# Attention and expert routing on one core: whole-pair slots, maxima ten pairs ahead, three stack buffers

## What is computed

```python
xl, xg = layer_norm(x, g_l, b_l), layer_norm(x, g_g, b_g)
glb   = mha(xg, ...)            # 16 heads of 8, softmax over the 256 tokens of a sequence
local = mha(xl[:, :32], ...)    # the same with its own weights, on tokens 0 to 31; 0 elsewhere
x1 = layernorm(x + local + glb)
# top-1 routing to 8 experts, capacity T/E = 1024, in token order
gates = softmax(x1 @ Wg); idx = argmax(gates); place = cumsum(one_hot(idx)) - 1
out = gates1 * (relu(x1 @ W1[idx] + b1) @ W2[idx] + b2)   # 0 for a token beyond the capacity
x = layernorm(x1 + out)
```

## Time and profile before

| | |
|---|---|
| median of three runs | 808.11 us |
| profiled execution | 806.47 us, span 804.4 us |
| attention steps 0 to 35 | 47.2 to 635 us |
| drain of the routing | to 665 us |
| expert stage | to the end |
| mean granted clock of TensorE | 0.917 |

### The profile page before, as it was taken

One profiled execution on the slowest core, in us unless ns is written; L12 is line 12 of the kernel. 1 busy time (PEld: TensorE's weight loads), 2 busy tenths in 40 slices (PEclk: granted clock), 3 DMA queues, 4 the chain that ended last, 5 costly groups with the idle time before them and its releaser, 6 DMA issues.

```text
span 804.4 us, 19344 instructions
## 1 busy us (share of the span) xinstructions
PE 698.3 (87%) x6502; PEld 352.4 (44%) x6502; DVE 571.7 (71%) x1703; ACT 489.6 (61%) x882; POOL 498.5 (62%) x1015
## 2 busy tenths in 40 slices
PE   1579779798999999999999999899999828999991
PEld 1434333343444444444444444344434415777771
DVE  5455577676988889889898898877888211666664
ACT  1335456575878677778787777777777614344340
POOL 4432323546677776777777878775765660667666
PEclk9755798888999999999999999999999958999996
DMA  3532576846254343552543534424431111343321
GB/s 89 174 127 60 158 188 141 207 108 211 63 175 145 107 154 86 156 166 83 173 142 111 155 109 138 154 75 146 128 114 51 32 29 51 103 128 95 98 76 35
DMA packets 145778, 95.36 MB, mean 119 GB/s; under 512 B 14404, under 2 KB 137885, under 8 KB 145680
## 3 DMA queue, kind: packets, MB, share of 16 engines
q1 hardware_dynamic: 139824, 85.35, 37.0%
q0 software_dynamic: 4096, 7.81, 3.0%
q10 hardware_dynamic: 1760, 0.96, 0.5%
HBM read 47.70 MB, written 45.74 MB: 116 GB/s over the span
## 4 chain that ended last, share of the span: by engine, by line
PE 62%; SPq 17%; DMA 7%; POOL 5%; issue 4%; DVE 3%; ACT 2%; POOLq 0%; ACTq 0%; DVEq 0%
PE ps_b L535 15%; PE ps_o L561 15%; SPq L328 8%; PE ps_a L1365 6%; DMA qs<-mT 5%; PE ps_b L1359 5%; SPq L357 5%; PE ps_f L476 3%; PE ps_f L481 3%; PE ps_f L471 2%; SPq L383 2%; POOL out L1479 2%; PE ps_a L512 2%; PE ps_f L1359 1%; PE ps_m L571 1%
## 5 line engine op out<-in xcount | busy, mean ns | idle before, releaser
L926 DVE TENSOR_REDUCE mx<-ps_a 128x2 f32<-128x512 f32 (+1 forms) x576 | 374.1, 656 | 119.0 <-PE ps_a L512 111.8
L759 ACT ACTIVATE prob<-ps_b 128x1024 f32<-128x1024 f32 (+1 forms) x288 | 281.1, 976 | 110.1 <-PE ps_b L535 97.0
L535 PE MATMUL ps_b<-qs,ks 59*128 59x256 bf16 (+1 forms) x1152 | 224.1, 277 | 32.1 <-DMA qs<-mT 29.6
L512 PE MATMUL ps_a<-ks,qs 56*128 56x256 bf16 (+1 forms) x1152 | 223.8, 279 | 7.2 <-DVE mx L926 4.8
L561 PE MATMUL ps_o<-prob,vp 128*32 128x256 f32 (+1 forms) x2304 | 184.8, 395 | 0.0
L535 PEld LDWEIGHTS ps_b<-qs,ks 59*128 59x128 bf16 x1152 | 67.0, 95 | 193.7 <-issue 113.5
L1153 POOL CAST mpart<-mx 128x16 bf16<-128x16 f32 x72 | 14.2, 197 | 123.5 <-DVE mx L926 123.2
L1217 POOL DMA_INDIRECT routed<-row,slot x64 | 67.3, 1051 | 31.5 <-issue 26.3
L1479 POOL DMA_INDIRECT out<-res,dest x64 | 64.8, 1013 | 34.2 <-DVE res L1454 19.1
L561 PEld LDWEIGHTS ps_o<-prob,vp 128*32 128x32 f32 x2304 | 46.8, 111 | 61.8 <-issue 54.9
L512 PEld LDWEIGHTS ps_a<-ks,qs 56*128 56x128 bf16 x1152 | 65.2, 96 | 12.9 <-DVE mx L926 8.7
(11 more groups left out here) (122 smaller groups left out, 1043.2 us busy)
## 6 DMA issues: line engine op xcount, KB each, us to landing
qs<-q_stack SPq DMA_DIRECT2D x144, 96.0 KB
ks<-k_stack SPq DMA_DIRECT2D x144, 96.0 KB
q_stack<-part SPq DMA_DIRECT2D x18, 384.0 KB
k_stack<-part SPq DMA_DIRECT2D x18, 384.0 KB
q_stack<-part SPq DMA_DIRECT2D x18, 256.0 KB
k_stack<-part SPq DMA_DIRECT2D x18, 256.0 KB
routed<-empty SPq DMA_DIRECT2D x8, 520.0 KB, 6.4
rows_sb<-routed SPq DMA_DIRECT2D x16, 260.0 KB, 3.8
```

What stands on the lines that cost most here:

```text
L512: ins = nc.tensor.matmul(ps_a[:, e, qt * S:qt * S + keys.stop - keys.start], qs[half, h, hp, qt * P:(qt + 1) * P], ks[half, h, hp, keys], ...
L535: ins = nc.tensor.matmul(ps_b[:, exp_bank(hp, e), kt * n:(kt + 1) * n], ks[half, u % 2, hp, kt * P:(kt + 1) * P], qs[half, u % 2, hp, quer ...
L759: nc.scalar.activation(prob[:, hp, 0:2 * n].rearrange("p (a n) -> p a n", a=2), src, ACT.Exp).then_inc(exp_done, 1)
L926: nc.vector.reduce_max(mx[:, u % 2, :, col], ps_a[:, e].rearrange("p (t k) -> p t k", t=2)[:, :, 0:k], axis=AX).then_inc(max_done, 1)
```

## The change

- Stacks: qs and ks have three buffers; load_stack(u) loads a whole unit with four DMAs, two steps ahead, and the mask rows are placed in four DMAs instead of eight.
- Maxima run LEAD = 10 head pairs ahead of the exponentials instead of 8.
- TensorE: the slot of a head pair is both score halves (eight matmuls), then one filler. The filler's work is spread anew over eight slots.
- Order: SP places the second maxima first, then loads the whole stack, then xr; store_stacks moves to the end of odd steps. GpSimd does scatter, bias_residual(u), split_max(u + 1, 0), the rows, the input's work, split_max(u + 1, 1), queue_places. The other engines' orders move to match.
- Small: the token counts use bf16 matmuls and accumulate the first tile's total in PSUM; oN and x1 are copied out of PSUM together (turned_T); queue_places has three operations instead of six; row numbers advance in place.

```diff
+LEAD = 10
-    qs = sb("qs", [P, 2, NH // 2, S], BF16)
-    ks = sb("ks", [P, 2, NH // 2, S], BF16)
+    qs = sb("qs", [P, 3, NH // 2, S], BF16)
+    ks = sb("ks", [P, 3, NH // 2, S], BF16)
...
-        def load_stack(u, half):
...
+        def load_stack(u):
+
+            b, h, p = u % 3, u % 2, u // 2
+            wait(sp, scores, 8 * (u - 2))
...
+                src = stack[p, :, :, h * S:(h + 1) * S].rearrange("(g e d) t n -> e (d t) g n", e=2, d=DH)
                 for e in range(2):
...
+                    sp.dma_start(dst[HALF * e:HALF * e + STACK, b], src[e]).then_inc(stack_loaded[b], 16)
...
         def step(u):
             p = first_pair(u)
-            if there(u + 1):
-                load_stack(u + 1, 1)
-            if u % 2 == 0 and u >= 2 and u // 2 + 1 < NPAIR:
-                store_stacks(u // 2 + 1)
             if there(u):
                 place_max(u, 1)
+            if there(u + 2):
+                load_stack(u + 2)
+            if there(u):
                 load_xr(u)
...
+            if there(u + 1):
+                place_max(u + 1, 0)
+            if u % 2 == 1 and (u + 1) // 2 + 1 < NPAIR:
+                store_stacks((u + 1) // 2 + 1)
             if p is not None and p + 2 < NPAIR:
                 load_x(p + 2)
-            if there(u + 2):
-                load_stack(u + 2, 0)
-            if there(u + 1):
-                place_max(u + 1, 0)
```

TensorE's filler, and its loop:

```diff
+            if hp == 0:
+                if there(u - 1):
+                    p_v(u - 1, 2, 1)
+                    p_v(u - 1, 3, 0)
                 if there(u):
+                    pe.wait_ge(mT_ready, 2 * u + 1)
                     wait(pe, y_ready, u - 1)
...
                     turn_max(u, 1)
+            if hp == 1:
+                if there(u - 1):
+                    p_v(u - 1, 3, 1)
+                inputs_early(u, 0)
+            if hp == 2:
+                inputs_early(u, 1)
...
+                    turn_o(u - 1)
+            if hp == 3:
                 if there(u):
+                    p_v(u, 0, 0)
                 if there(u + 1):
                     if there(u - 1):
                         pe.wait_ge(o_normed, u)
...
                     turn_max(u + 1, 0)
+            if hp == 4:
+                if there(u):
+                    p_v(u, 0, 1)
+                    p_v(u, 1, 0)
+                inputs_late(u, 0)
+            if hp == 5:
...
+                    count_tokens(u - 3)
+            if hp == 6:
...
         for u in range(U + 4):
             for hp in range(8):
-                for e in range(2):
-                    score_half(u, hp, e)
-                    fill(u, hp, e)
+                score_half(u, hp, 0)
+                score_half(u, hp, 1)
+                fill(u, hp)
```

VectorE (pick_place stands before the last slot's maxima) and GpSimd:

```diff
+            if at == (7, 0) and routes(u - 3):
                 pick_place(u - 3)
...
+                    if there(n // 8):
+                        take_max(n // 8, n % 8, e)
...
         def step(u):
             first, second = first_pair(u), second_pair(u)
-            if there(u):
-                split_max(u, 1)
             if routes(u - 4):
                 scatter(u - 4)
+            if there(u):
+                bias_residual(u)
+            if there(u + 1):
+                split_max(u + 1, 0)
             if routes(u - 2):
                 deviation(u - 2)
                 norm_rows(u - 2)
-            if there(u + 1):
-                split_max(u + 1, 0)
-            if routes(u - 3):
-                queue_places(u - 3)
-            if there(u):
-                bias_residual(u)
             if first is not None and first + 1 < NPAIR:
                 input_deviation(first + 1)
                 normalize_input(first + 1)
             if second is not None:
                 third_part(second)
+            if there(u + 1):
+                split_max(u + 1, 1)
+            if routes(u - 3):
+                queue_places(u - 3)
```

More of the change, by code:

```diff
@@ L771, in copy_o, with copy_turned @@
             nc.scalar.copy(oT[:], ps_o[:]).then_inc(oT_ready, 1)
-        def copy_oNT(u):
-            act.wait_ge(oN_turned, u + 1)
-            wait(act, projected, u)
-            nc.scalar.copy(oNT[:], ps_m[:, 0:S]).then_inc(oNT_ready, 1)
-        def copy_x1T(u):
-            g = batch(u)
-            act.wait_ge(x1_turned, g + 1)
-            wait(act, logits_ready, g)
-            nc.scalar.copy(x1T[:], ps_m[:, S:2 * S]).then_inc(x1T_ready, 1)
+        def copy_turned(u):
+            first, end = (0 if there(u - 1) else S), (2 * S if routes(u - 2) else S)
+            if there(u - 1):
+                act.wait_ge(oN_turned, u)
+                wait(act, projected, u - 1)
+            if routes(u - 2):
+                act.wait_ge(x1_turned, batch(u - 2) + 1)
+                wait(act, logits_ready, batch(u - 2))
+            nc.scalar.copy(turned_T[:, first:end], ps_m[:, first:end]).then_inc(turned_copied, 1)
         def norm_again(u):
@@ L813, in copy_counts @@
             act.wait_ge(counted, g + 1)
-            wait(act, places_ready, g)
-            nc.scalar.copy(count[:].rearrange("p a t e -> p (a t e)"), ps_m[:, 0:4 * E]).then_inc(counts_copied, 1)
+            wait(act, place_chain.sem, place_chain.steps * g)
+            nc.scalar.copy(count[:].rearrange("p a e -> p (a e)"), ps_m[:, 0:3 * E]).then_inc(counts_copied, 1)
         def step(u):
@@ L879, in _ @@
         copy_bv()
+        for g in range(3):
+            nc.scalar.activation(row[:, g, :, D + 1], c["tokid"][:], ACT.Copy, bias=float(g * S)).then_inc(row_numbered, 1)
         copy_max(0, 0)
@@ L1022, in fill @@
             first, second = first_pair(u), second_pair(u)
-            then = second + 2 if second is not None and second + 2 < NPAIR else None
+            early = second + 2 if second is not None and second + 2 < NPAIR else None
+            late = first + 1 if first is not None and AHEAD + 1 < first + 1 < NPAIR else None
             at = (hp, e)
-            if at == (0, 1):
+            if at == (0, 0):
                 if there(u - 2):
@@ L1047, in fill @@
+            if at == (2, 0):
+                if routes(u - 3):
+                    expert_mask(u - 3)
+                if routes(u - 2):
+                    mean_variance(u - 2)
+                if late is not None:
+                    input_stats(late, (2, 3))
+            if at == (3, 0) and there(u - 1):
                 invert_denominators(u - 1)
-            if at == (4, 1) and there(u - 1):
                 norm_o(u - 1)
-            if at == (5, 0) and then is not None:
-                input_stats(then, (0, 1))
@@ L1052, in fill @@
[L1052 to L1068 removed]
+            if at == (4, 0):
+                if second is not None:
+                    take_rest_k(second)
+                if late is not None:
+                    input_variance(late)
@@ L1251, in _ @@
         split_max(0, 0)
+        split_max(0, 1)
         for u in range(U + 4):
```

297 lines of the change are left out of this document (135 added, 162 removed).

## The result

The change makes the kernel slower: 1018.89 us (median of 4 runs, 1017.52 to 1020.1) against 807.48 us for the kernel before beside it, a ratio of 1.265 (95% interval 1.2586 to 1.2715). 966 us had been forecast, within 870 to 1060. The sign, the mechanism and nearly every mark in the profile came as written; the size was 53 us short.

A forecast was written before the change was run, and what follows sets the result against it. TensorE bounds the kernel before, VectorE a tenth behind. A loop through the xr load, lost clock and GpSimd's tail make batch steps 21.2 us: 746 against 588, +158, +1 for start and end, so 966 us, range 870 to 1060.

The forecast's parts named there:

- The loop closes in every step: GpSimd's wait for xr delays split_max and turn_max(u+1, 0): TensorE stands 4 to 5 us in every step.
- when xr is there: Input rows' arrival for GpSimd's bias_residual: issues end at T + 6.85, landing takes 2.0 us, so T + 8.9.
- T: The start of a step's pair 0, from which the prediction counts times within the step.
- four local steps: Steps with shorter slots but the same loop, slower xr landing and low clock: 19.5 us each, 78 together.
- Second half at the lower clock: TensorE after the stall: 7.7 us of second half plus 2.1 us clock loss, bounds 0 and 4.05.
- GpSimd's tail: GpSimd from xr wait to places in input-normalising steps: 11.3 us; 1.5 us more to next scores, 21.7 us a step.
- Boundaries: TensorE's fillers, sixteen to eight per step: saves 1.4 us a step, bounds 0.6 and 1.4.
- The DMA stalls go: TensorE's waits for maxima placed into qs: all but the first go, some 27 us and the low clock behind them.
- high end of 25 us a step: Issues 3.4, landing 2.75, clock loss 4.05 all at once: some 1090 us, called unlikely; range stopped at 1060.
- third rival: Clock stays low through the steps: 24.5 us a step, about 1065 us; chance 0.08.
- first rival: At bias_residual's wait, xr isn't late and the kernel is faster: 742 us; chance 0.08.
- VectorE's 14.0 us a step: In the first rival, VectorE's work becomes the bound, with some jitter 14.5 us for each of 36 steps.

The follow-up runs named there:

- the move alone: Kernel before with only bias_residual(u) moved directly behind scatter(u-4) on GpSimd: 981.56 us, ratio 1.21.
- second kernel of experiment 2: Kernel after with load_xr put between place_max(u, 1) and load_stack(u+2) on SP: 913.76 us, ratio 1.1201.
- experiment 4: Kernel after with nine extra f32 matmuls in the filler of pair 3, ahead of turn_max(u + 1, 0): 1035.95 us, ratio 1.2713.
- version of 783.5 us: Kernel after with GpSimd's queue_places before split_max(u+1,1), then bias_residual, scatter last; VectorE's picks and beyond_capacity in the next step: 783.49 us, ratio 0.9667.
- experiment 6: Version of 783.5 us with TensorE's order as before (four scores, part of the filler, four scores, the rest): 832.15 us, ratio 1.0294.

## Why the prediction was right, and where its sizes were off

- *The loop closes in every step.* Right: 36 waits for xr, 35 of TensorE for mpart; the move alone makes the loss in the kernel before, and undoing it, on GpSimd or on SP, takes nearly all of it back. The prediction's marks (no wait for qs<-mT, VectorE's wait for the places in about every second step, 20 times, the clock at 0.50 in part of each step) were all there. Their counts came as written, not their lengths: GpSimd's waits for xr are 8.9 us each, where 5 to 6 were written, and TensorE's 6.2 us, where 4 to 5 were.
- *The term that was mis-sized: when xr is there.* I had T + 8.9. Measured from T = 390.89: turn_max at T + 1.82 (1.55 taken), the copy 0.70 (0.71), two issues 1.46 (1.49), stack 2.0 with the gap before it 2.1 (1.8; 2.9 in the step before), xr issues 1.4 (1.3), landing 2.80 (2.0 taken, bounds 1.74 to 2.75). Together T + 10.4 and, in the step before, later still. The landing was outside its bounds (3.0 us on average): the rows of before had no whole stack load in front of the input rows; the second kernel of experiment 2 shows 1.5 us without it. TensorE thus stands 6.2 us, not 4 to 5. This late start is 1.5 us or more in each step and makes most of the 53 us: the 28 batch steps take 22.8 us instead of 21.2, which is 45 us, and the four local steps 21.5 instead of 19.5, which is 8.
- *Second half at the lower clock.* Priced at 7.7 + 2.1 = 9.8 us; measured 9.2 us in the step shown (403.41 to 412.60) and, with turn_max left out, 9.8 us on average. The size is right, and experiment 4 gives 1.5 us of it back with most of the clock. But the price decided nothing: with the clock up, GpSimd's tail sets the same end.
- *GpSimd's tail.* 11.3 us predicted, 11.3 us measured, and the next pair 0 starts 1.2 us behind the places (1.5 taken).
- *Boundaries.* 1.4 us a step taken; what whole slots bring in place is 0.3 to 0.85 us. The error hardly shows in the result: TensorE's first half ends in the stall, and experiment 4 shows that a shorter second half doesn't shorten the step.
- *The DMA stalls go.* Right: 29.6 us of waits for qs<-mT before, none of TensorE's matmuls after, 9.4 us in the version of 783.5 us. But that version waits 12.1 us for ks<-k_stack, the whole stack, where the kernel before waits 2.0 us, so only some 10 of its 24 us of span are DMA waits. How the gain divides wasn't measured. It needs the whole slots: undoing them (experiment 6) costs some 50 us and leaves the kernel slower than before, though it waits only 8.8 us for these two DMAs.
- *Two sums at the edge.* By the prediction's own way (35 equal steps and a last one of 14 us) the high end of 25 us a step gives some 1108 us, not 1090, and the third rival's 24.5 us gives 1090, not 1065. Neither moves the forecast or its range.
- *The first rival, 742 us with xr in time.* It could not have come even with the loop gone: behind it stood the second loop (816 us), and with that gone as well 783 us, with TensorE waiting for VectorE's maxima; that VectorE's pace is what is left is argued, not shown. I had VectorE's 14.0 us a step as a bound but not the order in which it meets GpSimd.

## What to carry to other kernels

Before an instruction that waits for a load is moved up in an in-order queue, follow the load back: if it is issued behind something of the same step that this queue's later work releases, the wait is a loop through every queue between, and its length is added to each step. Ask the same of the last instruction of a step, because a loop that is broken shows the next one. And a saving on the busiest engine is worth only what the second busiest lets through: here 0.3 to 0.85 of the 1.4 us that I had estimated.

## What the runs showed of the hardware that I had not expected

- Input rows landed 1.5 to 1.7 us after their last issue in nearly all plain steps with no stack load ahead of them, and 2.6 to 3.3 us with 768 KB of it just issued.
- With an indirect scatter on GpSimd in progress, ScalarE's start on a finished TensorE product came up to 1.8 us after it instead of 0.3 us, in many steps 0.33 to 0.47 us after the scatter's end; with the scatter elsewhere it came after 0.31 us. Two kernels with the same overlap (before and after) show none of it.
- With most of a 6 us stall filled by matmuls the clock held at 1.00 through the second half in 15 of the 22 steps read, which then took 8.0 us instead of 9.3 to 10.8; in the others it fell to 0.50 for some 3 us. No time was gained.
